# Ternary up projection: exact signs times two float32r parts of the input, the scale inside the ReLU, the low-rank term kept as 48 stacked rows

## The reference

```python
def _bitlinear(x, w_latent):
    scale = clip(mean(abs(w_latent), axis=1, keepdims=True), 1e-05, None)
    tern = clip(round(w_latent / scale), -1.0, 1.0)
    return x @ (tern * scale).T
h = _bitlinear(x, w_fc) + gate * (x @ v.T @ fast_b.T @ u.T)   # w_fc (1024, 256), u (1024, 16), v (16, 256)
r = jnp.maximum(h, 0.0)
return _bitlinear(r * r, w_proj)                               # w_proj (256, 1024)
```

## Time and profile before

| | |
|---|---|
| time, median of 3 runs (range) | 1096.81 us (1096.51 to 1098.58) |
| profiled execution, span from first to last instruction | 1094.8 us |
| PE matmul | 1019.2 us busy, 93% |
| DVE | 782.0 us, 71% |
| ACT | 607.7 us, 56% |
| POOL | 331.8 us, 30% |
| mean granted clock of PE | 0.975 |

### The profile page before, as it was taken

One profiled execution on the slowest core, in us unless ns is written; L12 is line 12 of the kernel. 1 busy time (PEld: TensorE's weight loads), 2 busy tenths in 40 slices (PEclk: granted clock), 3 DMA queues, 4 the chain that ended last, 5 costly groups with the idle time before them and its releaser, 6 DMA issues.

```text
span 1094.8 us, 20748 instructions
## 1 busy us (share of the span) xinstructions
PE 1019.2 (93%) x7648; PEld 601.0 (55%) x7648; DVE 782.0 (71%) x1337; ACT 607.7 (56%) x1191; POOL 331.8 (30%) x724
## 2 busy tenths in 40 slices
PE   5999989999999999999988898989898999999998
PEld 3675666433333333333344665648677676576865
DVE  4786577689999999999723747546536756887565
ACT  2665554478888888888853123131222456556543
POOL 3422111001010343344103334373366433530000
PEclk9999999889999999999998997999999999999999
DMA  7302221451221212212125100021344301100000
GB/s 213 70 16 88 87 68 66 144 188 44 75 71 48 70 49 69 79 45 70 47 67 191 34 15 10 20 77 44 101 155 132 100 31 49 44 25 1 16 18 26
DMA packets 97578, 75.67 MB, mean 69 GB/s; under 512 B 49806, under 2 KB 87483, under 8 KB 97223
## 3 DMA queue, kind: packets, MB, share of 16 engines
q1 hardware_dynamic: 94407, 65.95, 20.0%
q0 software_dynamic: 3072, 8.39, 2.4%
HBM read 42.94 MB, written 30.93 MB: 67 GB/s over the span
## 4 chain that ended last, share of the span: by engine, by line
PE 65%; DVE 10%; DMA 8%; issue 5%; POOL 4%; ACT 4%; SPq 3%; POOLq 0%; DVEq 0%; ACTq 0%
PE OUT L855 15%; PE TR L855 14%; PE OUT L1090 9%; PE TR L861 8%; PE TR L1079 7%; DMA head_q<-MT 7%; PE OUT L1079 3%; PE TR L931 3%; PE SCR L915 2%; POOL dispatched L2038 2%; SPq L697 2%; ACT PTS L1298 2%; PE SCR L908 2%; DVE small L1486 1%; PE OUT L861 1%
## 5 line engine op out<-in xcount | busy, mean ns | idle before, releaser
L1555 DVE TENSOR_REDUCE small<-SCR 128x1 f32<-128x1024 f32 x256 | 308.5, 1223 | 26.2 <-PE SCR L962 20.3
L1396 ACT ACTIVATE shared<-TR 128x512 f32<-128x512 f32 x352 | 200.1, 597 | 38.8 <-PE TR L1079 30.7
L962 PE MATMUL SCR<-head_k,head_q 48*128 48x512 f32 x512 | 193.9, 456 | 2.7 <-DVE P L1531 2.7
L1090 PE MATMUL OUT<-shared,HM 128*32 128x256 f32 x2048 | 165.3, 394 | 1.2 <-ACT shared L1396 0.4
L1079 PE MATMUL TR<-head_q,head_k 51*128 51x512 f32 x352 | 149.7, 463 | 0.9 <-issue 0.6
L1919 POOL TENSOR_SCALAR small<-small 128x1 f32<-128x1 f32 x112 | 27.7, 247 | 346.7 <-DVE small L1487 344.5
L855 PE MATMUL TR<-xT,fifo 128*128 128x512 f32 x224 | 105.8, 629 | 1.1 <-ACT xT L1276 1.0
L1396 ACT ACTIVATE shared<-OUT 128x512 f32<-128x512 f32 x160 | 95.8, 599 | 19.3 <-PE OUT L1079 17.6
L1079 PEld LDWEIGHTS TR<-head_q,head_k 51*128 51x128 f32 x352 | 60.6, 186 | 76.4 <-ACT shared L1396 56.5
L1276 ACT ACTIVATE xT<-TR 128x256 f32<-128x256 f32 x96 | 35.4, 381 | 111.5 <-PE TR L861 108.6
L1090 PEld LDWEIGHTS OUT<-shared,HM 128*32 128x32 f32 x2048 | 41.4, 108 | 93.1 <-ACT shared L1396 57.6
(11 more groups left out here) (241 smaller groups left out, 1860.3 us busy)
## 6 DMA issues: line engine op xcount, KB each, us to landing
pieces<-pieces SPq DMA_DIRECT2D x16, 512.0 KB, 2.7
HM<-dispatched SPq DMA_DIRECT2D x46, 128.0 KB
expert_out<-HM SPq DMA_DIRECT2D x46, 128.0 KB
dispatched<-HB SPq DMA_DIRECT2D x6, 768.0 KB, 4.0
head_q<-pieces SPq DMA_DIRECT2D x32, 128.0 KB
head_k<-pieces SPq DMA_DIRECT2D x32, 128.0 KB
shared<-in_L_ffn_w SPq DMA_DIRECT2D x4, 1024.0 KB, 12.0
x<-TOK SPq DMA_DIRECT2D x16, 128.0 KB, 1.7
```

The costliest lines, as they stand in the source:

```text
L962: ins = nc.tensor.matmul(SQ[kt % 2][:, hf, :], QX[n % 2][rows, kt * 128:(kt + 1) * 128], KX[n % 2][rows, hf * 512:(hf + 1) * 512], start=T ...
L1090: ins = nc.tensor.matmul(PV[32 * g:32 * g + 32, 0:256], VH[:, n % 2, kt, :], PTB[:, kt % 2, g * 256:(g + 1) * 256], start=(kt == 0), stop= ...
L1396: nc.scalar.activation(PTB[:, kt % 2, hf * 512:(hf + 1) * 512], ring_bank("t_scores", n, kt, hf), ACT.Exp, scale=DH ** -0.5).then_inc(st_d ...
L1555: nc.vector.tensor_reduce(nm[:, n % 2, kt:kt + 1], SQ[kt % 2].rearrange("p h n -> p (h n)"), AX, ALU.max, negate=True).then_inc(sq_done.se ...
```

## The change

The ternary weight now holds the bare signs, -1, 0 or 1, which float32r holds exactly. The input of the layer is split into a high float32r part (XWH, named ternary_in_high in the rows) and a low one (XWL, ternary_in_low), as FP already does with its input. The row scale moves into the ReLU's scale operand. The low-rank term isn't multiplied out: u, multiplied by gate / scale and split in two, is transposed to fcL (low_rank_out), 48 rows x 1024; x times (fast_b v) becomes YS (low_rank_mid), 48 rows x 512 tokens of a block; and FC adds one matmul over these 48 rows.

Step by step:
- GG, UT and FL leave part "a". UT returns in part "c" with eight transposes of the split u, between DN.6 and RK.1, and two copies on ACT.
- POOL no longer scales the signs; it splits u in part "b" (`low_rank_weights`). DVE computes gate / scale in two operations. In part "w" DVE copies the signs instead of adding them; PE does two small products of v and fast_b, ACT makes two copies and DVE one subtraction, which leave GH and GL.
- LT.t becomes LW.t: two transposes into an OUT bank, ACT's copy to XWH, DVE's subtraction to XWL, which frees the bank.
- YP.k is new, one for each block: PE waits until DVE is through the block's LW, then six float32r matmuls of 512 columns into one TR bank; ACT copies twice, DVE subtracts 16 x 512 elements; FC.k waits for this.
- FC.k: five float32r matmuls for each of the 8 output tiles, in place of two fp32 products.

The core of the diff:

```diff
+    "LW": dict(out=1, hi=1),
+    "YP": dict(tr=1, low_rank=1),
...
-PJ.3 LT.2 PN.3 CB.8 E.6 PV.5 CT.4 CG.10 S.7 LT.3 T.6 CB.9 OT.5 CB.10 DM.8 DM.9 E.7 FC.0 CG.11 PV.6 CG.12 L3.8 PJ.4
+PJ.3 LW.2 PN.3 CB.8 E.6 PV.5 CT.4 CG.10 S.7 LW.3 YP.0 T.6 CB.9 OT.5 CB.10 DM.8 DM.9 E.7 FC.0 CG.11 PV.6 CG.12 L3.8
...
-            def low_rank_product():
-                at.copied("UT")
-                at.copied("GG")
-                for k in range(KD):
-                    for hf in range(2):
-                        product(tr_bank(tl), [(G_sb[:, k * 128:(k + 1) * 128], uT[:, hf * 512:(hf + 1) * 512])])\
-                            .then_inc(tr_full.sem, 1)
...
+                def ternary_input(t):
+                    pe.wait_ge(tok_ready.sem, tl.after(tok_ready, "PN", t))
+                    bank = out_bank(tl)
+                    transposes(bank, [TOK[:, t % 2, k * 128:(k + 1) * 128] for k in range(KD)]).then_inc(out_full.sem, 1)
+
+                def low_rank_middle(k):
+                    pe.wait_ge(out_done.sem, tl.after_block(out_done, "LW", k))
+                    pe.wait_ge(g_ready, 1)
+                    bank = tr_bank(tl)
+                    product(bank[0:3 * R, :], [(g[:, f, :, :].rearrange("p c r -> p (c r)"), x[:, f, :])
+                                               for f in range(KD) for g, x in ((GH, XWH), (GH, XWL), (GL, XWH))])\
+                        .then_inc(tr_full.sem, 1)
+
                 def ternary_up(k):
-                    at.block_copied("LT", k)
+                    at.copied("UT")
+                    pe.wait_ge(y_ready.sem, tl.after(y_ready, "YP", k))
                     for m in range(MF):
-                        at.feature_major(fcT, xTs, m)
+                        ms_ = slice(m * 128, (m + 1) * 128)
+                        bank = tr_bank(tl)
+                        product(bank, [(fcT[:, f, ms_], x[:, f, :]) for f in range(KD) for x in (XWH, XWL)]
+                                + [(fcL[:, ms_], YS[:, :])]).then_inc(tr_full.sem, 1)
...
         @block.scalar
-                        nc.scalar.activation(r, bank, ACT.Relu).then_inc(tr_done.sem, 1)
+                        nc.scalar.activation(r, bank, ACT.Relu, scale=wscale[:, 0, m:m + 1]).then_inc(tr_done.sem, 1)
...
+                def low_rank_middle(k):
+                    bank = emptied(tl)
+                    nc.scalar.activation(YF, bank[2 * R:3 * R, :], ACT.Copy)
+                    nc.scalar.activation(YS[:, :], bank[0:3 * R, :], ACT.Copy).then_inc(tr_done.sem, 1)
...
         @block.vector
+                def ternary_input(t):
+                    bank = filled(tl)
+                    dve.wait_ge(xh_ready.sem, tl.next(xh_ready))
+                    c = t % BT * 128
+                    signal_out(tl, nc.vector.tensor_tensor(
+                        XWL[:, :, c:c + 128], bank[:, 0:256].rearrange("p (k n) -> p k n", k=KD),
+                        XWH[:, :, c:c + 128].bitcast(F32), ALU.subtract))
+
+                def low_rank_middle(k):
+                    dve.wait_ge(tr_done.sem, tl.next(tr_done))
+                    low = YS[2 * R:3 * R, :]
+                    nc.vector.tensor_tensor(low, YF, low.bitcast(F32), ALU.subtract).then_inc(y_ready.sem, 1)
```

More of the change, by code:

```diff
@@ L188, in attention_order @@
             before(("T", t), ("S", t + 2))
-            before(("LT", t), ("PN", t + 2))
+            before((last, t), ("PN", t + 2))
     for t in tiles:
@@ L245, in schedule_c @@
     order, before = parsed(ORDER_C)
-    attention_order(before, range(T))
+    attention_order(before, range(T), "LW")
     for t in range(T):
@@ L265, in schedule_c @@
         before(("FO", t), ("FC", 0))
-        before(("SO", t), ("LT", 0))
+        before(("SO", t), ("LW", 0))
+        before(("FO", t), ("LW", 0))
+        before(("LW", t), ("YP", t // BT))
+        before(("L2", t), ("UT",))
         before(("RT", t), ("FC", 0))
@@ L272, in schedule_c @@
             before((a, i - 2), (b, i))
+    before(("UT",), ("FC", 0))
     for k in range(T // BT):
+        before(("YP", k), ("FC", k))
+        for i in range(B * NS):
+            before(("UP", i), ("YP", k))
         before(("FI", k), ("L3", 0))
@@ L1145, in _ @@
                         .then_inc(tr_full.sem, 1)
+            pe.wait_ge(d_low, 16 * 4)
+            bank = tr_bank(tl)
+            for k in range(KD):
+                ins = nc.tensor.matmul(bank[:, k * R:(k + 1) * R], v_sb[:, k * 128:(k + 1) * 128], fbT, start=True, stop=True)
+            ins.then_inc(tr_full.sem, 1)
             pe.wait_ge(diag_ready, 1)
@@ L1417, in _ @@
                                          bank.rearrange("p (c n) -> p c n", c=4), ACT.Copy).then_inc(tr_done.sem, 1)
+            bank = emptied(tl)[:, 0:KD * R].rearrange("p (k r) -> p k r", k=KD)
+            nc.scalar.activation(GF, bank, ACT.Copy)
+            nc.scalar.activation(GH[:, :, :, :], bank.unsqueeze(2).to_broadcast([128, KD, 3, R]), ACT.Copy)\
+                .then_inc(tr_done.sem, 1)
             tl = Tally("c")
@@ L1433, in gates_exp, with low_rank_weights @@
                     nc.scalar.activation(pr_, lg, ACT.Exp, scale=-1.0).then_inc(gate_exp.sem, 1)
+                def low_rank_weights():
+                    for hf in range(2):
+                        bank = emptied(tl)
+                        nc.scalar.activation(fcL[:, hf * 512:(hf + 1) * 512], bank[0:3 * R, :], ACT.Copy)\
+                            .then_inc(tr_done.sem, 1)
+                def ternary_input(t):
+                    bank = OUT[:, tl.slot(out_full, 2), :]
+                    act.wait_ge(out_full.sem, tl.next(out_full))
+                    c = t % BT * 128
+                    nc.scalar.activation(XWH[:, :, c:c + 128], bank[:, 0:256].rearrange("p (k n) -> p k n", k=KD), ACT.Copy)\
+                        .then_inc(xh_ready.sem, 1)
+                def low_rank_middle(k):
+                    bank = emptied(tl)
+                    nc.scalar.activation(YF, bank[2 * R:3 * R, :], ACT.Copy)
+                    nc.scalar.activation(YS[:, :], bank[0:3 * R, :], ACT.Copy).then_inc(tr_done.sem, 1)
                 def ternary_up(k):
@@ L1830, in projected_norm @@
                     if t >= 2:
-                        left(tl, "LT", t - 2)
+                        dve.wait_ge(out_full.sem, tl.after(out_full, "LW", t - 2))
                     normalised(tl, chain, ("PJ", t), X[:, t, :], TOK[:, t % 2, :]).then_inc(tok_ready.sem, 1)
```

129 lines of the change are left out of this document (69 added, 60 removed).

## The result

The changed kernel takes 1117.82 us, the median of 4 runs (1115.82 to 1120.73); the kernel before took 1096.66 us beside it. The ratio is 1.0195, with a 95% interval of 1.0162 to 1.0227: slower by 21 us. The forecast was 1105.5 us with a range of 1091 to 1113. The direction was right, the size was not.

A forecast was written before the change was run, and what follows sets the result against it. PE was taken to bound the kernel, busy 1019.2 of 1094.8 us, with DVE limiting FC's gain at 1.33 us a tile. The terms summed to +8.7: span 1103.5, time 1105.5 us, range 1091 to 1113.

The forecast's parts named there:

- FC itself: FC's output tiles: 1.25 us on PE, under DVE's 1.33, so from 1.75 to 1.33; at most 3.4 us back a block.
- the dear case: FC's tiles at 0.28 us a matmul: 1.40 us a tile, 2.2 us dearer over the four blocks.
- The tail: FC.3 to FP.13: FC.3 and its wait fall from 16.1 to 12.8 us, +3.7 in front; net +0.4, bounds -2 and +3.
- The OUT ring: LW holds an OUT bank until DVE has subtracted: +1.6 us at DN.41, +0.4 for the others, bounds 0 to +3.
- YP.0: Block 0: PE idle 4.7 us for DVE's LW.3; FC.0 ends 2.9 us later on PE, bounds +1 and +5.
- The clock's +1.5: Behind YP.0's idle 4.7 us the granted clock falls to 0.50: +1.5 us, bounds 0 and +4.
- YP.1 and YP.2: YP.1, with OT.11: S.13 starts 4.9 us later, net +3.3 by OT.11; YP.2 nearly covered by FP.5 and FP.7, +0.3.
- OT.11: Behind FC.1: waits for LW.8's subtraction to free its bank, 1011.86 becomes 1015.2; net +3.3 with YP.1, bounds 0 and +5.
- The start: Start of the self-attention loop without GG, FL and UT: DVE's maxima become last to arrive; -3.1 us, bounds 0 and -4.9.
- (b): Rival: clock falls at YP.0 and again at YP.1 or OT.11, 4 to 6 us each; 1110 to 1116 us, chance 0.15.
- Rival (a): The waits are absorbed, FC worth 3.1 to 3.4 us a block: 1088.7, or 1080.0 if PE alone sets time; together 0.22.

The follow-up runs named there:

- full_rows: Changed kernel with low-rank operands 128 rows high, rows 48 to 127 zero, so all five FC matmuls have equal rows: 1120.86 us, ratio 1.0168 to the kernel before.
- lw_via_tr: Changed kernel with LW in a TR bank that ACT empties with two copies, DVE subtracting from the copy: 1114.48 us, ratio 1.0115 to the kernel before.
- pairs: Changed kernel with the 48-row matmul first in odd tiles, so two 48-row matmuls stand side by side: 1118.21 us, ratio 1.0163 to the kernel before.
- before_no_fold: Kernel before without GG, UT and FL, the low-rank term left out of the output: 1094.60 us, ratio 0.9957 to the kernel before.
- yp_late: Changed kernel with YP.0, YP.1 and YP.2 each moved behind two or three other steps: 1122.59 us, ratio 1.0224 to the kernel before.
- before_tail: Kernel before with FP waiting for the hidden tiles one by one instead of for all eight: 1095.69 us, ratio 0.9942 to the kernel before.

## Why the prediction was wrong, step by step

- **FC itself: the step that failed.** "I take 0.25, near the longer row: 1.25 us a tile, under DVE's 1.33." Both rows were of matmuls in a row of equal height. Measured are 0.23 for such ones and 1.56 a tile with the 48-row matmul among them. Not even the dear case, 1.40, was dear enough. full_rows prices it at 4.5 us, or 5.6 without the tail. What DVE can do was right: 1.33 in full_rows. The scale inside the ReLU was put at nothing and cost 0.09 us of ACT a tile.
- **The tail.** "The 2.14 us before FP.13 left it at 1.00." So I put nothing for the clock there. Behind 2.23 us it fell, and the changed kernel lost 1.5 us. The sum of this term is wrong as well: 0.9 + 0.38 + 0.42 + 0.2 + 1.5 is 3.4 and not 3.7.
- **The OUT ring** was mis-sized. The wait that I named first was right to 0.1 (1.67 before DN.41 against 1.6), and OT.10's 1.40 against 1.5. LW.15's 0.85 had its 0.9 in the tail's term. I then put 0.4 for all the others. But the two-bank ring had shifted for every step behind an LW: PJ.3 waited 1.05 us and LW.4 1.30, and behind the late DVE S.10 and S.11 waited 1.19 and 0.59 for banks of the scores. lw_via_tr prices LW in this ring at 9.0 us in all.
- **YP.0** was right in its mechanism: a wait of 4.46 us against 4.7, released by DVE's ternary_in_low, with a granted clock of 0.51 from 928 to 930. The times don't agree by themselves: FC.0's first multiply came at 937.10, near the 937.8 forecast, but only because the changed kernel was 3.5 us earlier at PJ.0. Counted from there it came 7.2 us later than before, where 4.4 for YP.0 and 2.0 for LW were put. The clock's +1.5 was about right here: the six matmuls took 2.40 us, those of YP.1 at the full clock 1.43.
- **YP.1 and YP.2** waited 1.35 and 1.00; for YP.2 with its matmuls I had put 0.3, as if the steps behind it could hide a wait ahead of it. Between the end of FC.1 and the start of FC.2 the delay grew by 5.1 us, and by 5.0 between FC.2 and FC.3.
- **OT.11** waited for DVE's LW.8, as forecast, but only 1.43 us, since PE itself came later through FC.1: the slow tile hid a part of this wait, and full_rows showed it again (2.44). The net delay from the end of FC.0 to OT.11 was 7.3 us where 3.3 were forecast; the slow tile, LW.4 and the two waits for scores are in it.
- **The start** was right in its mechanism, PE waiting for DVE's maxima in FL's place (2.28 us). That the number agrees, -3.1 forecast and 215.44 to 212.16, -3.3, is in part luck: the other kernels without FL began the loop between 212.63 and 217.29.
- **The rivals.** The time lies just above (b), but its mechanism, a second fall at YP.1 or OT.11, did not come: the clock was 1.00 from 998 to 1010 and from 1022 to 1026. It fell at YP.0 and in the tail. Rival (a), that PE absorbs the waits, is refuted by the waits of after.
The forecast span was 1103.5 and the profiled one is 1113.5. Ahead of PJ.0 the kernel came 3.5 us earlier where the terms for that part give 1.7, so the stretch was off by 11.8 us and not by 10. Counted from PJ.0, PE was later than before by 7.2 us at the end of FC.0, 14.5 at OT.11 and 20.7 at FP.13, and the end by 22.2; the terms, with the clock's, give 6.4, 9.7, 10.4 and 10.4. Of the 11.8 the tile is 5.6 and the tail's clock 1.5 by experiments. The other 4.7 go with the waits on the OUT and SCR rings, YP.2 and YP.3, which no single run divides further.

## What to carry to other kernels

A matmul of another height in a chain of 128-row ones costs more than its columns: pad it to the common height where the rows are free, or put those of one height side by side. Before a step takes a bank of a ring, ask which engine empties that ring and how long its queue is; count the ring anew for every later step. When PE's work shrinks under what DVE and ACT need for the same tile, the gain ends at their rate, and the wait behind the last tile grows (2.14 us before, 3.09 in full_rows). A finer wait there was worth more than the change. Before a forecast time is compared with a measured one, count both from the same event.

## What was not expected of the hardware

- A change of row count, 128 to 48 or back, cost about 0.2 us at the full clock: (1.56 - 5 x 0.23) / 2. The tile of pairs confirms it.
- A ReLU of 128 x 512 with a scale for each partition took 0.69 us on ACT where the one without took 0.60; I had put it at nothing. With the square's 0.63 ACT needs 1.32 a tile, as much as DVE, so a faster DVE alone would gain nothing.
- The clock fell behind a wait of 2.23 us of PE, which followed 15 us with 12.6 us of work (1086 to 1101), and didn't behind 2.14 us that followed a gapless FC. This came again: ahead of FP.13 it held in both profiles with the wait of 2.14 (before, before_no_fold) and fell in all four with 2.23 (after, pairs, yp_late, lw_via_tr) and all four with 3.09 to 3.34. The rows don't tell whether the length of the wait or the work ahead of it decides. In before_tail it fell at the end of part "a" with no gap ahead of it, so a wait isn't the only cause.
